# A gated attention layer with routed experts on one core: expert rows in full tiles of 128 and one 64-row tile per expert

## What is computed

```python
x = x + tanh(g_xattn[0]) * xattn(layernorm(x), ctx, seg_id, Wq, Wkv, Wo)
gate_probs = softmax(einsum('bsh,eh->bse', ln, gate_w))       # ln = layernorm(x), 8 experts
top_v, top_i = top_k(gate_probs, 2)
for e in range(8):
    h = silu(einsum('bsh,hf->bsf', ln, w1[e]) + b1[e])        # 256 -> 1024
    y = einsum('bsf,fh->bsh', h, w2[e]) + b2[e]               # 1024 -> 256
    out = out + y * comb_w[..., e:e + 1]                      # top_v where e was taken, else 0
x = x + tanh(g_ffn[0]) * out
```

## Time and profile before

| | |
|---|---|
| median of three runs | 337.86 us |
| time of the profiled execution | 338.57 us |
| its span | 336.8 us |
| mean granted clock of TensorE | 0.988 |
| TensorE busy (matmul) | 311.4 us, 92% |
| VectorE, ScalarE, GpSimd busy | 246.7, 195.3, 200.2 us |
| upward products (line 1159) | 1776 |
| downward products (lines 1173, 1174, 1178, 1179) | 592 |

### The profile page before, as it was taken

The page is one execution under the profiler, slowest core; times in us unless marked ns, Lnnn a source line. Parts: engine busy times, 40 slices in busy tenths (PEclk is TensorE's granted clock), DMA queues, the critical chain, the costliest instruction groups (busy, mean ns, idle before and its releaser), DMA issues.

```text
span 336.8 us, 11243 instructions
## 1 busy us (share of the span) xinstructions
PE 311.4 (92%) x3305; PEld 253.5 (75%) x3305; DVE 246.7 (73%) x581; ACT 195.3 (58%) x550; POOL 200.2 (59%) x223
## 2 busy tenths in 40 slices
PE   8688989999998888999999999999999998999990
PEld 7447879889887677778888877887877876868760
DVE  5648998889988967676878778687776877455551
ACT  2432466766554555757676666666676675453530
POOL 2466798997864052265665756666576665565413
PEclk9999999999999997999999999999999999999997
DMA  7799999999899928245655464654535536264222
GB/s 247 237 353 419 399 415 405 413 402 411 292 378 385 321 52 189 51 66 82 72 75 87 67 89 63 83 81 69 93 57 90 76 72 96 49 90 73 37 32 34
DMA packets 51098, 58.97 MB, mean 175 GB/s; under 512 B 24424, under 2 KB 45120, under 8 KB 48864
## 3 DMA queue, kind: packets, MB, share of 16 engines
q0 software_dynamic: 9408, 26.63, 33.5%
q1 hardware_dynamic: 36320, 28.22, 27.9%
q10 hardware_dynamic: 5312, 3.37, 3.2%
HBM read 43.32 MB, written 10.16 MB: 159 GB/s over the span
## 4 chain that ended last, share of the span: by engine, by line
PE 69%; POOL 11%; issue 8%; DVE 6%; DMA 2%; ACT 2%; POOLq 0%; ACTq 0%; DVEq 0%
PE ps L1159 29%; PE ps L1173 17%; PE ps L1174 8%; PE ps L995 4%; PE ps L1004 2%; PE ps L1179 2%; POOL sel L512 2%; PE ps L908 2%; POOL w_parts L512 2%; POOL sel L544 1%; POOL w_parts L544 1%; PE ps L1033 1%; DMA sel<-sel 1%; PE ps L1178 1%; DMA sel<-tokens_split,sel 1%
## 5 line engine op out<-in xcount | busy, mean ns | idle before, releaser
L1159 PEld LDWEIGHTS ps<-sel,w_parts 128*128 x1776 | 121.9, 99 | 35.9 <-issue 4.2
L1159 PE MATMUL ps<-sel,w_parts 128*128 128x128 f16 x1776 | 142.9, 221 | 2.6 <-DMA sel<-sel 1.3
L632 POOL DMA_INDIRECT out<-sel x37 | 59.8, 1615 | 78.6 <-ACT sel L871 56.0
L885 ACT ACTIVATE sel<-ps,b1T 128x128 f32<-128x128 f32 x296 | 83.4, 367 | 36.0 <-PE ps L1159 34.3
L1173 PE MATMUL ps<-w_parts,sel 128*128 x259 | 96.0, 380 | 0.6 <-issue 0.3
L1174 PE MATMUL ps<-w_parts,sel 128*128 x259 | 70.6, 273 | 0.0
L1556 DVE SCALAR_TENSOR_TENSOR w_parts<-w_parts (+1 forms) x32 | 39.2, 1231 | 31.4 <-ACT w_parts L854 31.3
L624 POOL DMA_INDIRECT sel<-tokens_split,sel x37 | 43.6, 1180 | 16.1 <-DVE sel L1538 9.8
L1571 DVE SCALAR_TENSOR_TENSOR sel<-sel 128x512 f16<-128x512 f32 x74 | 51.2, 692 | 2.5
L1569 DVE TENSOR_SCALAR sel<-sel 128x512 f16<-128x512 f32 x74 | 32.1, 434 | 17.6 <-ACT sel L885 17.5
L619 POOL TENSOR_TENSOR sel<-sel 128x1 f32<-128x1 f32 x37 | 38.2, 1033 | 6.4 <-DMA sel<-sel 6.4
(11 more groups left out here) (228 smaller groups left out, 424.2 us busy)
## 6 DMA issues: line engine op xcount, KB each, us to landing
w_parts<-in_L_ffn_w SPq DMA_DIRECT2D x16, 1024.0 KB, 12.3
out<-xs SPq DMA_DIRECT2D x16, 128.0 KB, 9.5
tokens_split<-xsplit ACTq DMA_DIRECT2D x13, 128.0 KB, 5.9
xs<-in_x ACTq DMA_DIRECT2D x2, 512.0 KB, 7.1
xs<-in_x SPq DMA_DIRECT2D x2, 512.0 KB, 6.2
near_rows<-w_parts SPq DMA_DIRECT2D x4, 256.0 KB, 9.2
xs<-in_L_ffn_b SPq DMA_DIRECT2D x1, 1024.0 KB, 6.8
sel<-tokens_split,sel POOLq DMA_INDIRECT x37
```

Source lines behind the costliest of these rows:

```text
L632: pool.indirect_dma_start(out_rows, bass.IndirectOffsetOnAxis(slot_row[:, at(q - 1)], 0), y_sb[(k + 3) % 4], None, compute_op=ALU.add).the ...
L885: act.activation(h32[n][:, c * P:c * P + P], ps_h[n][:, c * P:c * P + P], ACT.Silu, bias=biases[:, c:c + 1], scale=1.0 / (X_SCALE * W_SCALE))\
L1159: mm = pe.matmul(ps_h[n][:, c * P:c * P + P], w, xx, start=(i == 0), stop=(i == len(products) - 1))
```

## The change

Each expert now has as many full tiles of 128 rows as it has (members + 63) / 128, rounded down, and one half tile of 64 rows for what remains (0 to 64 rows; it is run where nothing remains too). Full tiles number 28 (`SURE`) to 35 (`N_FULL`), half tiles eight. Both stand in one list of jobs: half tile r is job 4 + 4r, with three full tiles between two half tiles. Only full tiles from the 29th on are behind a condition.

For a half tile, the upward products and the Silu, the splitting and the indirect DMAs have 64 rows (the transposing DMA stays as it is). Its downward products have the weights as the stationary side, 128 output columns at a time, and 128 (high and low) or 64 hidden rows moving: four products a chunk. The result stands turned, so b2 is added from a turned copy (`b2T`, loaded by one more small DMA at the start), the sum is turned back by two f32 transposes (`half_rows`) into `ps_rows`, in the middle of the step after, and ScalarE scales from there.

The routing gets five more small operations of VectorE where rows get their places (`r_end`, `r_hop`, `r_over`), lists of 43 columns for 39, and, in steps -2 and 2 of the expert stage, tables and a list of their own for the half tiles (`half_tables`, `half_list`). GpSimd waits for that list before it gathers job 4. The order of weights and their splitting stay, with the waits on it moved to each tile (`weights_ready`).

```diff
+    N_FULL = (B * S * TOP_K + E * (HALF - 1)) // P
+    SURE = (B * S * TOP_K - E * HALF) // P
+    NL = N_FULL + E
+    JOBS = []
+    for f in range(N_FULL):
+        if f > 3 and f % 3 == 1 and len(JOBS) <= 4 * E:
+            JOBS.append((True, (f - 4) // 3))
+        JOBS.append((False, f))
+    NT, ALWAYS = len(JOBS), SURE + E
...
+            act.dma_start(b2_raw, b2.rearrange("e (c p) -> (e c) p", p=P)).then_inc(s["small_in"], 16)
...
+                        rows, column = rows_of(q + 4), list_column(q + 4)
+                        if q + 4 == JOBS.index((True, 0)):
+                            pool.wait_ge(s["rt"], RT_HALF)
                         wait(pool, "slot_w_ok", q + 1)
-                        pool.indirect_dma_start(xg[k], None, xd, bass.IndirectOffsetOnAxis(slot_row[:, at(q + 4)], 0))\
+                        pool.indirect_dma_start(xg[k][rows, :], None, xd,
+                                                bass.IndirectOffsetOnAxis(slot_row[rows, at(column)], 0))\
                             .then_inc(s[f"gathered{k}"], 16)
...
+                    if is_half(t):
+                        act.wait_ge(s["rows_ps"], JOBS[t][1] + 1)
+                    else:
+                        act.wait_ge(s["y_sum_ok"], t + 1)
...
+            def up_chunk(q, c, first):
+
+                n, wide = q % 2, HALF if is_half(q) else P
                 products = []
                 for kc in range(KC):
                     hi = weights_at(first, kc, 0, c * P, P)
                     lo = weights_at(first, kc, 1, c * P, P)
+                    products += [(hi, kc), (hi, KC + kc), (lo, kc)]
+                for i, (w, a) in enumerate(products):
+                    mm = pe.matmul(ps_h[n][:, c * P:c * P + wide], w, xT[n][:, a, 0:wide], start=(i == 0),
+                                   stop=(i == len(products) - 1))
...
+            def half_down_chunk(q, c, first):
+
+                n = q % 2
+                both, hi = h_both[n][:, :, c * P:c * P + HALF], h_hi[n][:, c * P:c * P + HALF]
+                for j in range(KC):
+                    sides = ps_y[n][:, j * P:j * P + P].rearrange("p (a r) -> p a r", a=2)
+                    column = c % 4 * D + j * P
+                    pe.matmul(sides, weights_at(first, KC - 4 + c // 4, 0, column, P), both,
+                              start=(c == 0 and j == 0), stop=False)
+                    mm = pe.matmul(ps_y[n][:, j * P:j * P + HALF], weights_at(first, KC - 4 + c // 4, 1, column, P), hi,
+                                   start=False, stop=(c == FC - 1 and j == KC - 1))
...
+            def half_rows(q):
+
+                r = JOBS[q][1]
+                pe.wait_ge(s["y_sum_ok"], q + 1)
+                if r > 0:
+                    pe.wait_ge(s["y_ok"], JOBS.index((True, r - 1)) + 1)
+                for j in range(KC):
+                    mm = pe.transpose(ps_rows[:, j * P:j * P + P], xn[:, q % 2, j * HALF:j * HALF + P], ident[:, :])
+                mm.then_inc(s["rows_ps"], 1)
...
+                    pe.matmul(ps_prev[:, 0:N_FULL], e_prev[:, :], e_own[:, :], start=True, stop=True)
+                    pe.wait_ge(s["half_tables"], 2)
+                    pe.matmul(ps_half[:, 0:E], e_pad[:, :], e_half[:, :], start=True, stop=True)
+                    pe.matmul(ps_half[:, E:2 * E], ones16[0:E, :], e_half[:, :], start=True, stop=True)\
                         .then_inc(s["prev_ps"], 1)
...
+                        if c == 3 and live(-2) and is_half(q - 2):
+                            half_rows(q - 2)
...
+            link(v.tensor_tensor(r_end[:, :], r_first[:, :], r_tf[:, :], ALU.add))
+            v.scalar_tensor_tensor(out=r_hop[:, :], in0=r_rank[:, :], scalar=float(N_FULL), in1=r_end[:, :],
+                                   op0=ALU.add, op1=ALU.subtract)
             dve.wait_ge(s["rt_ps"], 2)
+            link(v.scalar_tensor_tensor(out=r_over[:, :, :], in0=spread_mid(r_tf[:, :], T), scalar=float(P), in1=base,
+                                        op0=ALU.mult, op1=ALU.is_le))
+            v.scalar_tensor_tensor(out=r_from[:, :, :], in0=spread_mid(r_first[:, :], T), scalar=float(P), in1=base,
+                                   op0=ALU.mult, op1=ALU.add)
+            link(v.scalar_tensor_tensor(out=r_over[:, :, :], in0=r_over[:, :, :], scalar=float(P),
+                                        in1=spread_mid(r_hop[:, :], T), op0=ALU.mult, op1=ALU.mult))
+            link(v.tensor_tensor(r_from[:, :, :], r_from[:, :, :], r_over[:, :, :], ALU.add))
...
+            def half_list():
+
+                halves_listed = ps_list[:, N_FULL + 1:NL + 1]
+                link(v.scalar_tensor_tensor(out=h_pad[:, :], in0=ps_half[:, E:2 * E], scalar=0.5,
+                                            in1=tok_f[:, 0:1].to_broadcast([P, E]), op0=ALU.is_lt, op1=ALU.mult))
+                link(v.tensor_tensor(h_pad[:, :], h_pad[:, :], ps_half[:, 0:E], ALU.add))
+                link(v.scalar_tensor_tensor(out=h_pad[:, :], in0=halves_listed, scalar=0.5, in1=h_pad[:, :],
+                                            op0=ALU.is_lt, op1=ALU.mult))
+                link(v.scalar_tensor_tensor(out=slot_row[:, N_FULL:NL], in0=halves_listed, scalar=-1.0, in1=h_pad[:, :],
+                                            op0=ALU.add, op1=ALU.add))
...
                 if q == 2:
                     dve.wait_ge(s["prev_ps"], 1)
-                    link(v.tensor_copy(tile_p[:, 4:NT], ps_prev[:, 4:NT]))
+                    half_list()
+                    link(v.tensor_copy(tile_p[:, 4:N_FULL], ps_prev[:, 4:N_FULL]))
```

More of the change, by code:

```diff
@@ L51, in flamingo_layer @@
     FC = F // P
-    NT = T * TOP_K + E - 1
-    FULL = T * TOP_K
+    HALF = P // 2
+    N_FULL = (B * S * TOP_K + E * (HALF - 1)) // P
[7 more added lines that the diff above has]
+    NT, ALWAYS = len(JOBS), SURE + E
+    EVEN = [SURE // E + (r < SURE % E) for r in range(E)]
+    FIRST_AT = [sum(EVEN[0:r]) for r in range(E)]
+    assert NT == NL and JOBS.index((True, E - 1)) == 4 * E and JOBS[ALWAYS] == (False, SURE)
     N_TOK = B * S
@@ L61, in flamingo_layer @@
     UC = KC * F // 2
-    assert TPB == 4 and KC == 2 and FC == 8 and T == 16 and UNITS == 2 * T and D == 256
+    assert TPB == 4 and KC == 2 and FC == 8 and T == 16 and UNITS == 2 * T and D == 256 and N_FULL == 35 and SURE == 28
     XD = D + E
@@ L203, in flamingo_layer @@
         r_at = over(1024, 2, T, E)
+        r_over = over(896, T, E)
+        r_hop = sb("r_hop", [P, E], F32)
         r_slot = sb("r_slot", [P, 2, T], I32)
@@ L218, in flamingo_layer @@
         e_row = sb("e_row", [E, P], F16)
[L219 to L228, removed]
+        e_ended = sb("e_ended", [E, N_FULL], F16)
+        e_own = sb("e_own", [E, N_FULL], F16)
+        e_new = sb("e_new", [E, N_FULL], F16)
+        e_half = sb("e_half", [E, E], F16)
+        valid = over(1828, NL)
+        l_pad = over(1696, NL)
+        l_tile = over(1408, 3 * N_FULL)
+        h_pad = over(1520, E)
+        slot_row = over(1740, NL).bitcast(I32)
+        slot_w = over(1784, NL)
+        tile_e = over(1872, N_FULL).bitcast(I32)
+        tile_p = over(1908, N_FULL).bitcast(I32)
         tiles_i = sb("tiles_i", [P, 1], I32)
@@ L237, in flamingo_layer @@
         y_low = [xn[:, i, :] for i in range(2)]
+        y_turn = [xn[:, i, 0:KC * HALF].rearrange("p (j r) -> p j r", j=KC) for i in range(2)]
         h32 = [sel1[:, 1024 * i:1024 * i + 1024] for i in range(2)]
@@ L241, in flamingo_layer @@
         h_lo = [kv16[:, 2048 + 1024 * i:3072 + 1024 * i] for i in range(2)]
+        h_both = [kv16.rearrange("p (a x) -> p a x", a=2)[:, :, 1024 * i:1024 * i + 1024] for i in range(2)]
         ps = ctx.enter_context(nc.psum_tensor("ps", [P, 8, 512], F32))
@@ L464, in _ @@
             sp.wait_ge(s["out_in"], 16 * T)
-            wait(sp, "scattered", tiles * 16)
+            wait(sp, "scattered", tiles * 16 + E * 16)
             sp.sem_inc(s["unused"], 1)
```

260 lines of the change are left out of this document (161 added, 99 removed).

## The result

The changed kernel takes 381.0 us (median, 379.96 to 381.37) where the kernel before takes 337.6 in the same comparison: a ratio of 1.127, 95% interval 1.124 to 1.130. The forecast was 331.9 with a range of 326.4 to 341. So the sign was wrong, and the size by 49 us.

The account below looks back on a forecast made before the run. TensorE alone was taken to bound the expert stage. -37.0 + 21.1 + 1.8 + 2.0 + 1.4 + 0.2 + 3.0 + 2.0 - 0.5 = -6.0 us; 338.57 - 6.0 - 0.7 = 331.9 us, range 326.4 to 341.

Parts of the forecast that it names:

- 31 ns a short product: TensorE's 64-column products in half tiles: slower than 27.5 ns each, +1.8 us in all, bounds 0 and +5.8.
- four distinct ones: Register-made addresses in a half tile's downward chunk on TensorE: four, each taken for one instruction; 20.9 ns was the slow pace.
- The burst: Eight 39-column TensorE products with full 128 x 128 loads at 115.55 to 115.77 in the earlier trace: 27.5 ns a pair.
- Rival D: Half tiles on TensorE: weight loads set the pace, 4.4 us a half tile, 344 us; chance 0.07.
- -37.0 + 21.1 us by columns: TensorE's expert stage: seven full tiles go at 5.28 us each, eight half tiles of 2.64 us come.
- the wait before job 4: TensorE stalls before the first half tile, whose gather waits for the half list: +3.0 us (2.3 to 4.9).
- a fall of the clock after it: TensorE's clock falls to 1.2 GHz after the stall before job 4: +2.0 us (0 to 2.5).
- the routing: VectorE's chain of placing rows before the expert stage: more small operations and wider masks, +1.4 us (1.1 to 1.6).
- the turning back itself: Two f32 transposes on TensorE for each of eight half tiles: +2.0 us in all (1.8 to 3.0).
- TensorE's wait for the sum at the turning back: VectorE's sum comes 0.8 us into a step, TensorE needs it 2.6 us in: covered, so no cost.
- C: Rival: GpSimd's chain of scatters becomes the bound; at 5.1 us a job throughout, 341.7 us; chance 0.13.
- E: Rival: transposing DMAs come too late in the 16 short steps; all late +10 us, half +5, 337; chance 0.08.

Follow-up runs that it names:

- the fixed kernel: The changed kernel with every weight address written in as a constant for these inputs, so TensorE has no register additions or register loads: 339.7 us, 1.007 times the kernel before.

## Why the prediction was wrong

*What failed: the pace.* The prediction took +1.8 us for "31 ns a short product" with a high end of +5.8. That end came from 128 instructions at 20.9 ns, the stretch of the earlier trace rows, on the words that "four distinct ones" cost one instruction each like any other. The additions were counted rightly and priced wrongly, nearly six times too low. The row could not carry the price, for two reasons that could have been seen. The 20.9 ns are a mean over products and additions; if the 32 additions alone bear the 2.84 us, it is 89 ns each. And the 48 products of 298.65 follow a tile's downward products, 2.64 us in which only 8 additions are needed, so that TensorE's instructions can have run ahead; over the whole tile, 5.46 to 5.56 us for 40 additions, there is room for up to 0.139 us each. And the price itself was in the trace of the kernel before, in the view of the products' source line: the 31 additions of these products in 3.6 us, 0.12 us each, begun 1.4 us before the first of them. With 0.119 us the step with 64 additions is 7.6 us and not 4.0, eight times 3.6, and the half-up step, 40 additions, 4.76 and not 4.0: together 35 us.

*A term that was left out: loads of registers.* The rest lies at the ends of steps: 1.1 us behind each half tile's downward products (the 0.9 to 1.1 us idle before the next), and 0.1 to 0.9 in the full step ahead of them (6.13 for 5.28 here, 5.41 in the group after). There TensorE loads the registers that the addresses start from. One load for each half tile is new:

```profile
L1367 PEldq TENSOR_LOAD <-order_i x8: 534/538/548, 138.4 to 317.8; - x8
L1299 PEldq TENSOR_LOAD <-sel x9: 327/332/771, 123.9 to 344.4; - x9
```

In the changed kernel TensorE is idle for over 0.15 us 14 times after 150 us, 12.3 us in all, and every time such a load stands just before. In the kernel before that happens twice, for 1.5 us, since its instructions are ahead. The page puts most of these idle times down to VectorE's sum (L1776), but the sum that the products at 192.86 need is that of three tiles back, done by 186.8; between 191.6 and 192.8 stand the load, 0.54 us, and five more register and semaphore instructions. So the additions give 35 us and the loads some 11; the few that are left of the 49 lie in the first chunks of steps, 0.79 us for 0.66, and in the clock below.

*The burst was right and misled.* Short products with full loads do run at their columns' pace: 55 and 30 ns in the fixed kernel's chunk. Its addresses were fixed, as the prediction said itself; it then put its value near the burst and not near the case with registers.

*Rival D, at 344 us, was nearest and wrong in its mechanism.* Weight loads don't set the pace; the fixed kernel has every one of them.

*What held.* 30 full and 8 half tiles; 0.50 and 0.66 us a chunk and so -37.0 + 21.1 us by columns, in every step of the fixed kernels that has no wait and a clock of 1.00; the wait before job 4, 2.82 us for 3.0; a fall of the clock after it, with chunks of 0.95 to 0.96 us for 0.50 (1152 columns at 1.2 GHz) and a step 2.2 us too long for 2.0; a second fall at 166.75, behind the next idle time (0.96 us; as long ones later left the clock at 1.00), cost some 1.6 us more and was not forecast; the routing, from the last sum of `r_first` to the first gather 10.18 us (109.38 to 119.56) for 8.94 (111.20 to 120.14, the end in the earlier trace rows), +1.2 for +1.4; the turning back itself, 0.22 us. The first gather came at 119.56 and not near 121.5, because the first part ended 1.8 us earlier in this execution; so the +0.2 for one more small load can't be seen.

*What was called covered and isn't:* TensorE's wait for the sum at the turning back. In the changed kernel it is covered, because the step is slow. Once the additions are gone it costs 8.2 us. The 0.8 us to the sum were read beside a full tile's steps, and the rows showed no short one. They were also too few: the step was reckoned to start at 140.15, and the trace has its first product at 139.94, so 1.0 us.

*C and E didn't come.* GpSimd's scatters waited for the one before 15 times, 29.7 us in all, but TensorE has no wait that leads there; for the transposing DMA it waited once, before job 4. Without the additions the changed kernel is at 337 to 340 us, no faster than the kernel before as it was and slower than that kernel without its own additions (333.2). So with the pace put right the sign of the forecast is still wrong: the waits that follow VectorE take back the six us that the columns give.

## What to carry to other kernels

Count TensorE's register instructions a chunk, not its matmuls alone: a weight tile whose address is made at run time costs about 0.12 us of TensorE's instruction time here, more than two products of 128 columns, and a load of registers 0.3 to 0.5 us. Their rows are in the trace: ask for the source line of the products and look for `PEldq`. A change that halves the columns and keeps or raises the number of distinct addresses is slower as soon as that product is larger than the columns' time; find the slack before (here 0.60 of 0.66 us) by dividing a step's whole length, never a burst behind long products. A busy TensorE in the page may be an engine that waits for its own instructions: compare the spacing of products of different width, and where width makes no difference, it isn't the array.

## What the runs showed of the hardware

- An addition into a register on TensorE has a row of 32 ns, but one starts every 0.112 us at best and every 0.118 to 0.119 on average when nothing is ahead, at 5, 7 and 8 of them a chunk; eight to ten products of 64 to 512 columns fit beside them at no time of their own.
- A load of TensorE's registers takes 0.33 us (L1299) to 0.54 (L1367), and TensorE idles up to 1.1 us behind the longer one when nothing is ahead; the page names another engine for it.
- TensorE's instructions run ahead of its array: seven chunks of a half-up step run at the columns' 0.50 us (173.80 to 177.30, behind chunks of up to 1.28 us at the slow clock) before the additions show, and the first half tile's downward chunks began at 0.50 and ended at 0.96.
- The two changes of a chunk between a stationary side of 128 columns and one of 64 take 0.22 us together; widening the narrow one with useless columns gave 9.5 us back.
- Products of 64 columns with a full 128 x 128 weight load are 30 ns apart, those of 128 columns 55 ns. The Trainium skill ("TensorE: Matmul & The Clock Gate", Back-to-back issue gap) gives a stream of loads and 128-column products about 81 ns a product; the rows here at a granted clock of 1.00 say 55.
